# A two-layer Mamba and mixture-of-experts kernel: another order ahead of the first scan, blocks taken out a slot later, gate products one a slot in the second layer

## The reference, cut to what matters

```
xn = layernorm(x)
x = x + mamba0(xn) * silu(moe0(xn))      # layer 0
xn = layernorm(x)
x = x + mamba1(xn) * silu(moe1(xn))      # layer 1

mamba0: x_in, z = xn @ W_in.T;  gate = silu(conv4(x_in)) * z
        delta = softplus(gate @ W_dt.T + b_dt);  B, C = gate @ W_xproj.T     (16 states)
        h = exp(delta * A) * h + delta * B * gate;  y = sum_n(h * C) + xn;  layernorm(y) @ W_out.T
moe0:   top-1 of 8 experts; the expert does relu(layernorm(x) @ W1 + b1) @ W2 + b2, times the gate
mamba1: 4 heads of 64 channels, 16 states each; x = silu(conv4(x_in)); B, C, dt per head;
        the same recurrence; y = (sum_n(h * C) + x * Dskip) * silu(z);  y @ out_proj.T
moe1:   all 8 experts: sum_e cw_e * (silu(xn @ w_gate_e) * (xn @ w_up_e)) @ w_down_e
```

## Time and profile before

| | us |
|---|---|
| median of three executions (684.86, 685.33, 688.0) | 685.33 |
| the profiled execution | 684.94 |
| its span, from the first to the last instruction | 683.2 |
| PE busy in the span | 576.1 (84%) |
| DVE busy | 585.9 (86%) |
| POOL busy | 533.4 (78%) |
| ACT busy | 451.9 (66%) |
| TensorE clock granted over the span, mean | 0.962 of full speed |

### The profile page before, as it was taken

How to read it: one execution, slowest core, us unless ns; L and a number is a source line. 1 busy time by engine, 2 the same in 40 slices (tenths; PEclk the granted TensorE clock), 3 DMA queues, 4 the chain that set the end, 5 groups by cost and what they waited for, 6 DMA issues and landing times. The chain is left out here.

```text
span 683.2 us, 8361 instructions
## 1 busy us (share of the span) xinstructions
PE 576.1 (84%) x2075; PEld 331.4 (49%) x2075; DVE 585.9 (86%) x921; ACT 451.9 (66%) x708; POOL 533.4 (78%) x431
## 2 busy tenths in 40 slices
PE   3646998889638957999999799999799999799997
PEld 2411676667214423644444454444354444566674
DVE  6899887879898979997879988988989788898995
ACT  4555676866724768757786766787665887766660
POOL 3456568665884577987998899999799999799991
PEclk9998999999877989999999999999999999999999
DMA  8087988997888677776667678657676867787970
GB/s 264 23 309 229 321 315 260 305 342 234 269 266 282 200 175 182 193 199 164 168 165 204 169 192 209 184 158 201 170 198 181 214 164 184 182 213 202 231 190 17
DMA packets 71216, 142.25 MB, mean 208 GB/s; under 512 B 8352, under 2 KB 37088, under 8 KB 71168
## 3 DMA queue, kind: packets, MB, share of 16 engines
q1 hardware_dynamic: 67984, 130.74, 68.1%
q0 software_dynamic: 3184, 10.98, 4.7%
HBM read 133.23 MB, written 8.45 MB: 207 GB/s over the span
## 5 line engine op out<-in xcount | busy, mean ns | idle before, releaser
L929 DVE TENSOR_TENSOR_SCAN state<-decay,bank 128x512 f32<-128x512 f32 x128 | 155.9, 1218 | 13.4 <-POOL product L1275 5.4
L2023 PE MATMUL bank<-xw,wu 128*128 128x512 f32 x256 | 133.0, 601 | 13.7 <-DVE hid L1059 13.5
L1275 POOL TENSOR_TENSOR product<-state,CB 128x512 f32<-128x512 f32 x90 | 116.8, 1297 | 17.7 <-DVE state L929 13.9
L1277 POOL TENSOR_TENSOR product<-product 128x512 f32<-128x512 f32 x90 | 119.8, 1332 | 7.1
L1676 ACT ACTIVATE sg<-bank 128x512 f32<-128x512 f32 x128 | 75.4, 597 | 65.7 <-PE bank L1913 56.9
L2041 PE MATMUL bank<-hid,wd 128*128 128x512 f32 x192 | 99.1, 597 | 6.0 <-DVE hid L1059 6.0
L1059 DVE TENSOR_TENSOR hid<-sg,bank 128x512 f32<-128x512 f32 x128 | 84.9, 665 | 21.8 <-PE bank L2023 20.2
L1925 PE MATMUL bank<-product,early 128*128 128x512 f32 x112 | 71.7, 739 | 33.6 <-POOL product L1320 14.6
L922 DVE TENSOR_TENSOR bank<-bank,CB 128x512 f32<-128x512 f32 x128 | 88.8, 694 | 12.8 <-DMA CB<-crow 10.9
L1596 ACT ACTIVATE decay<-delta,negA 128x510 f32<-128x510 f32 x128 | 82.5, 710 | 10.7 <-DVE delta L887 5.4
L1911 PE MATMUL bank<-XH,wh 128*128 128x512 f32 x128 | 73.5, 574 | 10.5 <-ACT sg L1676 3.7
(11 more groups left out here) (240 smaller groups left out, 1117.7 us busy)
## 6 DMA issues: line engine op xcount, KB each, us to landing
CB<-crow SPq DMA_DIRECT2D x256, 256.0 KB, 4.1
CB<-crow SPq DMA_DIRECT2D x44, 512.0 KB, 5.0
cwb<-cwrow SPq DMA_DIRECT2D x32, 256.0 KB, 4.6
szm<-crow SPq DMA_DIRECT2D x11, 512.0 KB, 5.3
cwb<-crow SPq DMA_DIRECT2D x9, 512.0 KB, 5.6
xw<-Wg_dram SPq DMA_DIRECT2D x8, 256.0 KB, 4.5
wd<-Wd_dram SPq DMA_DIRECT2D x8, 256.0 KB, 5.7
wu<-Wu_dram SPq DMA_DIRECT2D x8, 256.0 KB, 4.7
```

What stands on the lines that cost most here:

```text
L929: v.tensor_tensor_scan(state[:, c % RING, :], decay[:, PLACE[c], :], drive, 0.0, ALU.mult, ALU.add).then_inc(state_ready.sem, 1)
L1275: p.tensor_tensor(addend, state[:, c % RING, :], cs, ALU.mult).then_inc(state_used.sem, 1)
L1277: ins = p.tensor_tensor(product[:, m, :], product[:, m, :], addend, ALU.add)
L2023: t.matmul(bank[up_bank(i, u)][:, :], wu[:, e, 128 * f:128 * f + 128], xw[:, e % 2, :], start=True, stop=True).then_inc(up_ps.sem, 1)
```

## The change

It has four parts.

1. **Ahead of the first scan.** On ACT `th` comes ahead of two copies and the normalising of quarter 0, and `dt`, `row` and `ln` stand ahead of the router's Exp and of quarter 1. On DVE `xs`, `zx` and `rest` stand among the statistics, `delta` ahead of `route_choice`, and `route_slots` after slot 1 of the loop (ROUTE_AT = 1), where it was ahead of slot 0. Quarters 2 and 3 are normalised by POOL (8 tensor_scalar), behind `less` and ahead of the scatters. `fold_conv` goes from POOL's start to slot 6 (FOLD_AT = 6). PE's row product of the first pair has a bank of its own and waits no longer for `dt` to be read. SP loads gates 0 and 1 in slots 10 and 11 of its loop; they stood ahead of it.
2. **Blocks.** The first 11 blocks are taken out a slot later, behind the next chunk's drive and ahead of its scan.
3. **Gates.** In layer 1 PE does at most one or two gates in a slot, spread over the slots ahead of their use (GATE1_LAST, GATE1_AT); for e = 1 nothing moves.
4. **Silu.** ACT does two of an expert's four Silus in its first slot and two in its second, for all e but 1, and forms the decays behind them. No instruction comes between the two halves, so ACT's order of instructions in layer 1 is what it was; what moves is the gate for which the last Silus wait.

The core of the diff:

```diff
+GATE1_LAST = [-1, -1] + [k // FT * FT + (-1, -1, 0, 0)[k % FT] if k // FT == 1 else k - 2 for k in range(2, UNITS)]
+GATE1_AT = [k // FT * FT + (-1, 0, 0, 1)[k % FT] if k // FT in EXTRA else at for k, at in enumerate(GATE1_LAST)]
-RELU_AT, DOWN_AT, TAKE_AT = ([at + lag for at in UP_AT] for lag in (1, 3, 5))
+TAKE_AT = [at + (6 if b < 11 else 5) for b, at in enumerate(UP_AT)]
+ROUTE_AT, FOLD_AT = 1, 6
+GATE_LOAD_AT = [10, 11] + [at - 10 for at in SPLIT_AT[2:]]
...
             for g in range(CB_RING):
                 load_cb0(g)
-            load_gate(0)
-            load_gate(1)
...
-                for e in now(SPLIT_AT, s + 10):
-                    if e >= 2:
-                        load_gate(e)
+                for e in now(GATE_LOAD_AT, s):
+                    load_gate(e)
                 for g in range(CB_RING, PAIRS * N):
...
+            def second_norm(q):
+                pool.wait_ge(shift2_ready.sem, shift2_ready.at0(0, q + 1))
+                pool.wait_ge(xf_ready.sem, xf_ready.at0(0, q))
+                for k in range(TT):
+                    last = p.tensor_scalar(xf_rows[:, q, k, :], x_rows[:, q, k, :], rstd2[:, q, k:k + 1], shift2[:, q, k:k + 1], ALU.mult, ALU.add)
+                last.then_inc(xf_ready.sem, 1)
...
-            fold_conv()
             head0("less", 0)
+            second_norm(2)
+            second_norm(3)
             for s in range(PAIRS * UNITS):
                 slot0(s)
+                if s == FOLD_AT:
+                    fold_conv()
...
-                if u % FT == 0:
-                    for k in range(1 if more and u // FT in EXTRA else 2, FT):
-                        gate1(i, u + k)
-                if u % FT == FT - 1 and u + 1 < UNITS:
-                    for k in range(1 if more and (u + 1) // FT in EXTRA else 2):
-                        gate1(i, u + 1 + k)
+                for k in now(GATE1_AT if more else GATE1_LAST, u):
+                    gate1(i, k)
```

More of the change, by code:

```diff
@@ L533, in first_pair, with row_bank @@
             return isinstance(j, int) and j == 0
+        def row_bank(j):
+            return bank[DX_BANK if first_pair(j) else HEAD_BANK]
         def over_e(ap):
@@ L1163, in _ @@
             second_norm(0)
+            head0("xs", 0)
+            head0("zx", 0)
             second_stats(1)
-            head0("xs", 0)
             second_norm(1)
             second_stats(2)
-            head0("zx", 0)
+            second_norm(2)
             second_stats(3)
-            second_norm(2)
+            head0("rest", 0)
+            second_norm(3)
             route_logits()
-            second_norm(3)
-            head0("rest", 0)
+            head0("delta", 0)
             route_choice()
-            head0("delta", 0)
-            route_slots()
             for s in range(PAIRS * UNITS):
                 slot0(s)
+                if s == ROUTE_AT:
+                    route_slots()
             for u in range(FIRST_LATE):
@@ L1519, in head0 @@
                     act.wait_ge(rows_out[0].sem, rows_out[0].at0(j, 0))
-                    a.activation(rows[:, 0, :], hb[0:96, :], ACT.Copy).then_inc(head_read.sem, 1)
+                    a.activation(rows[:, 0, :], row_bank(j)[0:96, :], ACT.Copy).then_inc(head_read.sem, 1)
             def head1(name, j):
@@ L1686, in slot1 @@
                         head1({"x": "xs", "z": "sz"}[EXTRA[e][0]] + EXTRA[e][-1], i + 1)
-                    for f in range(FT):
+                    for f in range(FT if e == 1 else 2):
                         silu(i, u + f)
@@ L1690, in slot1 @@
                         late(u)
+                elif u % FT == 1 and e != 1:
+                    for f in range(2):
+                        silu(i, u + 1 + f)
+                    if late:
+                        late(u)
+                elif late:
+                    late(u)
+                if u % FT == (0 if e == 1 else 1):
                     for c in DECAYS1[e]:
                         form_decay(i, c)
-                elif late:
-                    late(u)
                 if u == (LATE if i else FIRST_LATE):
@@ L1724, in _ @@
             copy_x(1)
+            head0("th", 0)
             copy_x(2)
+            copy_x(3)
             second_norm(0)
-            head0("th", 0)
-            copy_x(3)
-            second_norm(1)
             head0("dt", 0)
+            head0("row", 0)
+            head0("ln", 0)
             act.wait_ge(lg0_ready.sem, lg0_ready.at0(0, 1))
             a.activation(lexp0, lg0, ACT.Exp).then_inc(lexp0_ready.sem, 1)
-            head0("row", 0)
-            head0("ln", 0)
             head0("delta", 0)
-            for g in range(AHEAD):
+            decay0(0)
+            decay0(1)
+            second_norm(1)
+            for g in range(2, AHEAD):
                 decay0(g)
@@ L1785, in head0 @@
             def head0(name, j):
-                pe.wait_ge(head_read.sem, head_read.at0(j, BANK0.index(name)))
+                apart = first_pair(j) and name == "row"
+                pe.wait_ge(head_read.sem, head_read.at0(j, BANK0.index("dt" if apart else name)))
                 if name == "xin":
@@ L2097, in _ @@
             turn(1)
+            head0("z", 0)
             logits(0)
-            head0("z", 0)
             logits(1)
@@ L2102, in _ @@
             turn(3)
+            head0("dt", 0)
+            head0("row", 0)
             logits(2)
             logits(3)
-            head0("dt", 0)
-            head0("row", 0)
             pe.wait_ge(late_in.sem, late_in.at0(0, 16 * 3))
```

14 lines of the change are left out of this document (7 added, 7 removed).

## The result

The changed kernel takes 699.99 us (median of four executions, 698.7 to 700.82); the kernel before, run beside it, 685.1 (683.38 to 688.0). The ratio is 1.0205, with a 95% interval of 1.0183 to 1.0227: the change costs 14.9 us by the medians and 14.0 by the ratio. The profiled execution has a span of 697.9 us, 14.7 more than that of before.

A forecast was written before the change was run, and what follows sets the result against it. The prediction took a chain through ACT, DVE and PE to bound the start, PE the blocks and POOL layer 1's pair middles. It summed 684.94 + 4.3 (block start) - 2.0 (takes) + 0.7 (layer 1) = 687.9 us, range 681.5 to 693.

The forecast's parts named there:

- The sign of the sum: Whole kernel: slower than before, 687.9 us against 684.94.
- the start of the blocks: Chunk 9's drive and PE's first block turn come later behind SP's wait: +4.3 us (2.7 to 6.3).
- layer 1: Moved gates and Silus: up to -2.5 us from shorter waits, up to +3 from ACT's lateness; taken as +0.7.
- That SP's wait swallows the lead: SP waits for `fold_conv` behind POOL's scatters, so DVE's 2.9 us lead becomes idle time before chunk 9's drive.
- POOL's first pack comes 3 us later and is not the last to arrive: Start of the blocks: the first block's pack on POOL is 3 us later, but something else arrives after it.
- The lead: Start of the kernel: DVE's second drive goes near 39.5 in place of 42.37, a lead of 2.9 us.
- The takes: Blocks: taking the first 11 out a slot later shortens DVE's waits for down products: -2.0 us (0 to -3.5).
- The rival: Layer 1: the last Silu is 1.5 us late on ACT, POOL waits once a pair, 4.5 in all: 691.7; chance 0.12.
- The gain by one gate fewer ahead of an up: Layer 1: waits for an up shrink by three products, 0.8 us; about -2.5 us at most in all.
- The wait doesn't bite: Start of the blocks: chunk 9's broadcast still comes in time, the stage gains 0 to 1 us: 683.1; chance 0.20.
- all of it is gained: The 2.9 lead reaches the blocks, takes give 2, POOL's layer 1 idle time goes (-2.5): 677.5; chance 0.08.
- The rival of the shared port: Start: POOL's moved normalising stretches DVE's work by 2.3 us, so `slot_of`, scatters and blocks come later: 690.2; chance 0.08.

The follow-up runs named there:

- experiment 2: The changed kernel with layer 1's gates back where PE did them before the change: 691.32 us (ratio 1.0089).
- experiment 6: The changed kernel with layer 1's gates as before and `fold_conv` on POOL between `less` and the normalising of quarters 2 and 3: 683.22 us (0.9982).
- experiment 10: The changed kernel with SP loading gates 0 and 1 in slot 14 in place of 10 and 11: 698.8 us (1.0187).
- experiment 5: The changed kernel with SP loading gates 0 and 1 in slots 20 and 21, `fold_conv` still behind the scatters: 695.74 us (1.0157).
- experiment 12: The changed kernel with `fold_conv` behind the first block's pack (slot 16) and gates 0 and 1 loaded in slots 24 and 25: 691.51 us (1.0092).
- experiment 4: The kernel before with only the first 11 takes a slot later: 682.57 us (0.9973).
- experiment 7: The kernel before with layer 1's gates spread as in the change for all experts but 5 and 6: 683.39 us (0.9977).
- experiment 11: The changed kernel with POOL loading the second block's pack three slots later: 699.89 us (1.0226).

## Why the prediction was right or wrong

687.9 us was forecast, 681.5 to 693, and 699.99 came. The sign of the sum was right, its size wrong by a factor of five. Two terms of the sum failed, the start of the blocks and layer 1; by the ratios of the experiments the three terms measured +7.3, -1.8 and +7.9, together 13.4 of the 14.0 us.

*That SP's wait swallows the lead* held up to the landing: `slot_of` done at 38.76 (38.5 forecast), scatters to 61.05 (61.1), gate 0 at 64.95 (64.4), chunk 9's drive at 69.95 (69.9 to 70.1). Some of the closeness is luck: PE's first product started 0.74 us earlier in this execution (8.93 against 9.67), `fold_conv` took 3.9 in place of 3.1, and chunk 9's broadcast, issued at 65.33 and not 64.6, landed in 4.6 and not 5.0.

*The size of that term* is the first step that failed: +4.3 (2.7 to 6.3) was forecast for the start of the blocks, and it was +8.1 at PE's first turn (77.20 against the 69.06 of the earlier trace rows) and, by experiments 2 and 6, 8.1 in time (7.3 by the ratios). Two estimates were wrong. The transfers behind the wait were given the median landing of each kind in the earlier trace rows, 5.0 and 6.6 us. These come from a run in which the transfers were spread, and here two gates, three broadcasts and two packs, 3.2 MB by the sizes of their rows, were asked for within 2.6 us (64.95 to 67.53), ahead of the block's read or, the second pack, as it was being issued; it took 9.7, and chunk 10's broadcast 8.9. The full engines are a part of that; by experiment 10 they aren't the whole. And "POOL's first pack comes 3 us later and is not the last to arrive" held only as long as SP's wait hid it: experiments 5 and 12 give it 4.2 us by itself.

*The lead* of 2.9 in the forecast was 2.7 in the traces, but against a late start of the kernel before; against the others it is 0.1 to 0.9. This step didn't change the forecast's sum, since the lead was forecast to be lost.

*The takes*, -2.0 (0 to -3.5) forecast, gave -1.8 by the ratio of experiment 4. Right.

*Layer 1*, +0.7 (-2.5 to +3) forecast, was +8.7 by the medians of experiment 2, +7.9 by the ratios: the second step that failed. The rival had the first half of the mechanism (the last Silu late, `dt0`, `z0` and `row1` behind it, POOL waiting for it) with a price of 1.5 a pair, 4.5 in all, and a chance of 0.12. The lateness is 3.0 us, not 1.5, at expert 5, since there the gate stands behind the head's `row1` too, which the forecast read off the order at an expert without such a step. ACT's idle time takes none of it up on the way to `row1`'s copy, and PE, which waits for that copy, stands still for 1.69 us. And the sum had no term for PE's clock, which it put at nothing without a reason: behind that wait it fell to half for 3.4 us at a time, four times in the first three pairs, which made PE late for DVE and DVE for POOL. The gain by one gate fewer ahead of an up was there, as forecast: 1.2 us at expert 4 of the first pair (between scans 80 and 82), and 1.6 in all in experiment 7.

*The rivals.* "The wait doesn't bite" and "all of it is gained" fell. The rival of the shared port, in which POOL's moved normalising stretches DVE's work by 2.3 us, fell as well: the eight instructions ran from 34.92 to 38.74, beside `route_slots`, and that took 3.2 us (35.59 to 38.76) where it took 2.9 in the earlier trace rows. L811, the 128x128 step that took 1.32 beside `less` in the kernel before, took 0.29 with nothing beside it; a 128x4 step of DVE (28.52) took 1.21 beside `less` now. The rule of the Trainium skill, "SBUF — State Buffer", "Who interferes with whom", agrees with the two long steps, each about as long as POOL's 1.26; that a row of POOL instructions of 0.44 us cost next to nothing is the measurement's to say, and by it the stretch is no longer than the instruction in the way.

## What to carry to other kernels

Before a piece of work is moved on one engine, look for whoever waits for its signal on the others, and on a queue that works in order count everything behind that wait, with the transfers at the landing times of a full queue rather than at the median. A step made late for TensorE costs more than its lateness where the clock falls behind the wait: look at the granted clock of the stretch after each short wait, in more than one execution, since the same wait of 1.69 us was followed by a fall in some pairs and not in others. And take the start of a profiled execution from more than one execution before a gain of 2 or 3 us is read off it.

## What the runs showed of the hardware

In layer 1 a wait of PE of 1.69 us, with the clock at full speed before it, was followed by a fall of the granted clock to half for 3.4 us in the first pair of the changed kernel and by none in the first pair of experiment 11; the same 12 products took 6.00 and 4.89 us. A pair with more falls lost more, by some 1.3 us a fall (an estimate from 24 pairs).

POOL's indirect transfers and SP's shared the 16 DMA engines here: one pack of 592 KB fewer on POOL's queue let a 128 KB read on SP's land 1.7 us earlier (8.0 in place of 9.7), while the engines moved 397 to 401 GB/s in 70 to 78 us.

PE's products at the start of an execution took either 1.07 or 1.95 us for eight at a shown clock of 1.00; it was 1.95 in 4 of 16 profiled executions. In the old order the longer time went with a second scan 1.9 us later, in the new order with no shift.
